# Four block owners packed into one word, read ahead of the marks; nine matmuls added to TensorE's stream at the end of attention

## The reference

```python
x = x + relu(attention(layernorm(x), ctx, ctx, mask) @ wo.T + wo_b)
h = layernorm(x)
weights, indices = gate(h)            # softmax over 32 experts, 4 of 8 groups, top 4 of 32
cw = scatter(weights, indices)        # [T, 32]
for e in range(32):
    y += cw[:, e] * ((silu(h @ w1[e] + b1[e]) * (h @ w3[e] + b3[e])) @ w2[e] + b2[e])
z = (silu(h @ sw1 + sb1) * (h @ sw3 + sb3)) @ sw2 + sb2
x = x + y + z
```

## Time and profile before

| | |
|---|---|
| time, median of 3 runs | 398.54 us (397.88 to 400.85) |
| time of the profiled execution | 398.79 us |
| its span, first to last instruction | 396.9 us |
| attention ends, the second part begins | about 159 us from the span's start |
| first row scatter to the last | 190.05 to about 231 us |
| marks landed | 239.7 us |
| first bias add of the block loop | 268.86 us |
| last bias add | 367.3 us |
| busy in the span | PE 288.5, DVE 222.1, POOL 181.8, ACT 147.2 us |

### The profile page before, as it was taken

One profiled execution on the slowest core, in us unless ns is written; L12 is line 12 of the kernel. 1 busy time (PEld: TensorE's weight loads), 2 busy tenths in 40 slices (PEclk: granted clock), 3 DMA queues, 4 the chain that ended last, 5 costly groups with the idle time before them and its releaser, 6 DMA issues.

```text
span 396.9 us, 7150 instructions
## 1 busy us (share of the span) xinstructions
PE 288.5 (73%) x2283; PEld 209.0 (53%) x2283; DVE 222.1 (56%) x702; ACT 147.2 (37%) x403; POOL 181.8 (46%) x188
## 2 busy tenths in 40 slices
PE   8899999999999994999910002207999999999200
PEld 3366666666666672947500002106778888888100
DVE  1778876777777775286940001004556666666277
ACT  1366666666667653231000000003444544444000
POOL 6466765756666750100677720001545555555400
PEclk9999999999999997589965555657999999999755
DMA  6868797787956000860133363001545555553394
GB/s 157 186 55 231 215 309 205 220 247 240 298 183 215 0 3 0 237 187 2 53 93 93 97 85 67 14 0 40 160 138 155 159 162 163 165 164 106 109 289 133
DMA packets 54013, 55.92 MB, mean 141 GB/s; under 512 B 18925, under 2 KB 45562, under 8 KB 53466
## 3 DMA queue, kind: packets, MB, share of 16 engines
q1 hardware_dynamic: 49610, 43.94, 40.4%
q0 software_dynamic: 4368, 11.52, 9.4%
HBM read 35.03 MB, written 20.41 MB: 140 GB/s over the span
## 4 chain that ended last, share of the span: by engine, by line
PE 24%; issue 19%; DVEq 6%; DVE 5%; DMA 3%; SPq 2%; POOL 1%; ACT 0%; POOLq 0%
PE ps L860 13%; PE ps L875 6%; DVEq L1078 6%; DVE x L1098 4%; PE ps L852 3%; PE ps L869 2%; DMA marks<-expert_rows 2%; SPq L735 1%; DMA b<-expert_out 1%; POOL expert_out L781 1%; DMA expert_out<-hs,to 1%; SPq L734 0%; DVE hh L1091 0%; ACT sg L932 0%; DVE hb L1085 0%
## 5 line engine op out<-in xcount | busy, mean ns | idle before, releaser
L286 POOL TENSOR_SCALAR z<-z,zmax 112x375 f32<-112x375 f32 x64 | 79.0, 1246 | 52.8 <-DVE zmax L546 52.8
L781 POOL DMA_INDIRECT expert_out<-hs,to x59 | 56.8, 962 | 84.9 <-DVE hs L1068 83.2
L546 DVE CUSTOM_DVE_ANT_0 z<-ps,mask_sb 112x375 f32<-112x375 f32 x128 | 62.5, 546 | 29.6 <-PE ps L365 29.6
L474 ACT ACTIVATE pT<-ps 125x336 f32<-125x336 f32 x128 | 50.7, 448 | 38.1 <-PE ps L342 37.7
L860 PE MATMUL ps<-w,xgT 128*128 x236 | 64.3, 396 | 0.5
L1085 DVE TENSOR_TENSOR hb<-ps,b 128x256 f32<-128x256 f32 x59 | 25.1, 425 | 60.1 <-issue 33.1
L342 PE MATMUL ps<-ident,z 112*125 112x112 f32 x384 | 56.6, 283 | 0.2 <-ACT pT L474 0.2
L852 PE MATMUL ps<-ident,xg 128*128 128x128 f32 x118 | 23.6, 285 | 45.4 <-issue 45.4
L342 PEld LDWEIGHTS ps<-ident,z 112*125 112x125 f32 x384 | 47.3, 188 | 15.4 <-ACT pT L474 7.3
L860 PEld LDWEIGHTS ps<-w,xgT 128*128 128x128 f32 x236 | 45.0, 197 | 11.0 <-issue 5.3
L776 POOL DMA_INDIRECT expert_rows<-normed,slots x32 | 32.0, 1000 | 39.1 <-DVE normed L1042 29.6
(11 more groups left out here) (156 smaller groups left out, 360.1 us busy)
## 6 DMA issues: line engine op xcount, KB each, us to landing
xg<-expert_rows SPq DMA_DIRECT2D x59, 128.0 KB
expert_rows<-zero SPq DMA_DIRECT2D x14, 512.0 KB, 10.0
w2s<-in_L_ffn_w SPq DMA_DIRECT2D x2, 2048.0 KB, 9.1
b<-in_L_ffn_b SPq DMA_DIRECT2D x2, 2048.0 KB, 12.9
b<-expert_out SPq DMA_DIRECT2D x8, 448.0 KB, 8.2
ctx_sb<-in_ctx SPq DMA_DIRECT2D x8, 375.0 KB
mask_sb<-in_mask_Bx1xSxS_ff SPq DMA_DIRECT2D x8, 164.1 KB, 2.4
expert_out<-hs,to POOLq DMA_INDIRECT x59
```

The costliest lines, as they stand in the source:

```text
L286: pool.tensor_scalar(z[:, n % RING, :], z[:, n % RING, :], zmax[:, n % RING:n % RING + 1], None, ALU.subtract).then_inc(by_pool, 1)
L474: nc.scalar.activation(pT[:, n % RING, :], ps[0:KP, T_BANK + at % 2, 0:KT * S], ACT.Exp).then_inc(ring_read, 1)
L546: nc.vector.tensor_tensor_reduce(out=z[:, n % RING, :], in0=ps[0:S, S_BANK + j, 0:SK], in1=mask_sb[:, b % 2, :], scale=-1.0 if j in ACT_HE ...
L781: pool.indirect_dma_start(ys, bass.IndirectOffsetOnAxis(ap=to[:, j:j + 1], axis=0), y_sb[:, j % 4, :], None).then_inc(y_sent[j % 4], 16)
```

## The change

Two parts. **Words:** the owners of four blocks are packed as digits of base 32 into one number below 32^4 (`word`, then `word_i` as integer). With 59 blocks there are NWORD = 15 words. Both engines read 15 words ahead of their loops and none in it; VectorE reads them in front of its wait for the marks. Each use of an owner now works it out from the word: `owner_of` shifts by 5, 10 or 15 bits and masks with 31, in front of the multiplication by the stride that `bass.ds` has had before. That is done for each of the two matmul calls of `up`, for `down`, and for the bias add. VectorE makes the words with four small memsets, one multiplication and one reduction more. PART, STEP and the rounding of NBLK keep their values (128, 32, 59). **Matmuls:** nine calls of `warm`, into a bank of PSUM whose scores have been read, stand between the last steps of attention on TensorE.

```diff
-    NBLK = (TOPK * T + E * (P - 1)) // P
-    LIM = -(-T // P)
+    PART = P
+    NBLK = -(-((TOPK * T + E * (PART - 1)) // PART) * PART // P)
+    NWORD = -(-NBLK * P // (4 * PART))
+    LIM = -(-T // PART)
+    STEP = 32
...
-                def warm(n):
+                def warm(n, bank=SUM_BANK):
...
+                pe.wait_ge(masked, HPQ * NQ)
+                warm(2, S_BANK)
                 turn_sums(B - 1)
+                warm(2, S_BANK)
                 turn_att(B - 1)
+                warm(1, S_BANK)
                 project(B - 1)
+                warm(4, S_BANK)
...
-            HELD = 44
+            def owner_of(words, n):
+                return (words[n // 4] >> (5 * (n % 4))) & (E - 1)
...
-                                               w13[:, k, bass.ds(own[j], 1), :].rearrange("p o c -> p (o c)"),
+                                               w13[:, k, bass.ds(owner_of(words, j), 1), :].rearrange("p o c -> p (o c)"),
...
-                                     w2s[:, bass.ds(own[j], 1), :].rearrange("p o c -> p (o c)"),
+                                     w2s[:, bass.ds(owner_of(words, j), 1), :].rearrange("p o c -> p (o c)"),
...
                 pe.wait_ge(table_ok, 1)
-                own = {j: pe.value_load(owner_i[0:1, j:j + 1], min_val=0, max_val=E - 1) for j in range(HELD)}
+                words = [pe.value_load(word_i[0:1, n:n + 1], min_val=0, max_val=E ** 4 - 1) for n in range(NWORD)]
...
-                    if j >= 2 and j - 2 + HELD < NBLK:
-
-                        own[j - 2 + HELD] = pe.value_load(owner_i[0:1, j - 2 + HELD:j - 1 + HELD], min_val=0, max_val=E - 1)
...
+                for f in range(4):
+                    nc.vector.memset(places5[:, f:f + 1], float(E ** f))
...
-                nc.vector.tensor_scalar(owner_i[:], owner[:], float(E - 1), None, ALU.min).then_inc(table_ok, 1)
+                chained(nc.vector.scalar_tensor_tensor(owner[:], owner[:], float(E - 1),
+                                                       places5[:].unsqueeze(1).to_broadcast([1, NWORD, 4]), ALU.min, ALU.mult))
+                chained(nc.vector.tensor_reduce(word[:], owner[:], AX.X, ALU.add))
+                nc.vector.tensor_copy(word_i[:], word[:]).then_inc(table_ok, 1)
...
+                dve.wait_ge(table_ok, 1)
+                words = [dve.value_load(word_i[0:1, n:n + 1], min_val=0, max_val=E ** 4 - 1) for n in range(NWORD)]
 
                 dve.wait_ge(marks_in, 16)
...
-                dve.wait_ge(table_ok, 1)
-                own = {j: dve.value_load(owner_i[0:1, j:j + 1], min_val=0, max_val=E - 1) for j in range(HELD)}
                 dve.wait_ge(scale_in, 16 * 2)
                 for j in range(NBLK + 3):
                     if j < NBLK:
-                        if j >= 1 and j - 1 + HELD < NBLK:
-                            own[j - 1 + HELD] = dve.value_load(owner_i[0:1, j - 1 + HELD:j + HELD], min_val=0, max_val=E - 1)
                         dve.wait_ge(up_done, j + 1)
                         TT(hb[:, j % 2, :], ps[:, U_BANKS[j % 2], 0:2 * INTER],
-                           b13[:, bass.ds(own[j], 1), :].rearrange("p o c -> p (o c)"), ALU.add).then_inc(biased, 1)
+                           b13[:, bass.ds(owner_of(words, j), 1), :].rearrange("p o c -> p (o c)"), ALU.add).then_inc(biased, 1)
```

More of the change, by code:

```diff
@@ L294, in _ @@
             def _(pe):
-                def warm(n):
+                def warm(n, bank=SUM_BANK):
                     for _ in range(n):
-                        nc.tensor.matmul(ps[:, SUM_BANK, :].rearrange("p (r c) -> p r c", c=P), ident[:],
+                        nc.tensor.matmul(ps[:, bank, :].rearrange("p (r c) -> p r c", c=P), ident[:],
                                          ident[:].unsqueeze(1).to_broadcast([P, BANK // P, P]), start=True, stop=True)
@@ L696, in experts @@
             cw = sbe("cw", [S, B, NE])
-            count1 = sbe("count1", [P, NBLK])
+            count1 = sbe("count1", [P, 4 * NWORD])
             copies = sbe("copies", [P, TOPK])
@@ L707, in experts @@
             gate = sbe("gate", [S, B, TOPK])
-            owner = sbe("owner", [1, NBLK])
-            owner_i = sbe("owner_i", [1, NBLK], I32)
+            owner = sbe("owner", [1, NWORD, 4])
+            word = sbe("word", [1, NWORD])
+            word_i = sbe("word_i", [1, NWORD], I32)
+            places5 = sbe("places5", [1, 4])
             hs = sbe("hs", [P, NSH, T])
@@ L958, in shared_h @@
                                                    sil[:, u % 2, :], ALU.add, ALU.mult).then_inc(hs_ok, 1)
-                chained(nc.vector.memset(over[:, 0:9, :], 1.0))
-                unit = over[:].rearrange("p e l -> p (e l)")[:, 0:NBLK]
+                for f in range(4):
+                    nc.vector.memset(places5[:, f:f + 1], float(E ** f))
+                chained(nc.vector.memset(over[:, 0:4 * NWORD // LIM + 1, :], 1.0))
+                unit = over[:].rearrange("p e l -> p (e l)")[:, 0:4 * NWORD]
                 chained(nc.vector.tensor_tensor_scan(count1[:], unit, unit, 0.0, ALU.mult, ALU.add))
                 chained(nc.vector.tensor_scalar(copies[:], count1[:, 0:TOPK], -1.0, None, ALU.add))
-                chained(nc.vector.tensor_scalar(full[:], count1[:, 0:LIM], -1.0, float(P), ALU.add, ALU.mult))
+                chained(nc.vector.tensor_scalar(full[:], count1[:, 0:LIM], -1.0, float(PART), ALU.add, ALU.mult))
                 dve.wait_ge(logits_ok, 1)
@@ L1033, in _ @@
                 chained(TT(blocks[:], ends[:], blocks[:], ALU.subtract))
-                chained(nc.vector.tensor_scalar(base1[:], blocks[:], float(P), 1.0, ALU.mult, ALU.add))
+                chained(nc.vector.tensor_scalar(base1[:], blocks[:], float(PART), 1.0, ALU.mult, ALU.add))
                 chained(TT(key[:], ps[0:S, 5, 0:B * E].rearrange("s (b e) -> s b e", e=E),
@@ L1042, in _ @@
                 nc.vector.tensor_scalar(normed[:, :, D:D + TOPK], best[:, :, 0:TOPK], -1.0, None, ALU.add).then_inc(slots_ok, 1)
-                for lo in range(0, NBLK, D * 4 // E):
-                    some = slice(lo, min(lo + D * 4 // E, NBLK))
+                for lo in range(0, 4 * NWORD, STEP):
+                    some = slice(lo, min(lo + STEP, 4 * NWORD))
                     n = some.stop - lo
@@ L1050, in _ @@
                                count1[0:1, some].unsqueeze(2).to_broadcast([1, n, E]), ALU.is_lt))
-                    chained(nc.vector.tensor_reduce(owner[:, some], passed, AX.X, ALU.add))
-                nc.vector.tensor_scalar(owner_i[:], owner[:], float(E - 1), None, ALU.min).then_inc(table_ok, 1)
+                    chained(nc.vector.tensor_reduce(owner[:].rearrange("p n f -> p (n f)")[:, some], passed, AX.X, ALU.add))
+                chained(nc.vector.scalar_tensor_tensor(owner[:], owner[:], float(E - 1),
+                                                       places5[:].unsqueeze(1).to_broadcast([1, NWORD, 4]), ALU.min, ALU.mult))
+                chained(nc.vector.tensor_reduce(word[:], owner[:], AX.X, ALU.add))
+                nc.vector.tensor_copy(word_i[:], word[:]).then_inc(table_ok, 1)
                 for r in range(TOPK):
```

## The result

The changed kernel takes **368.8 us** (median of four runs, 368.61 to 369.23) against 399.17 of the kernel before (four runs, 397.88 to 400.85): 0.926 of its time, interval 0.922 to 0.930. The profiled execution took 368.61 us, its span is 366.8 us. Of the kernels further down, words_only and dve_ahead each have one run in a slower state of the chip (373.88 and 371.10), which is left out of their times.

A forecast was written before the change was run, and what follows sets the result against it. It took GpSimd's scatters, VectorE's sequencer reading owners, then TensorE's block loop as the bound. Its terms gave 398.8 - 26.0 - 1.0 - 3.0 + 1.0 - 1.4 = 368.4 us, range 364.5 to 376.

The forecast's parts named there:

- Part 4: Shift and mask at each owner use in the block loop, taken as fused steps: plus 1.0 us, between 0 and 3.5.
- Part 5: Nine matmuls at attention's end: turn_sums later, +1.1; transposes and logits faster, -2.5; sum -1.4 us, between -2.5 and +1.1.
- Part 1: VectorE's owner reads moved ahead of the marks: first turn_h earlier by 26.0 us, between -25.2 and -26.7.
- Part 2: First blocks of the loop: less time with TensorE at half clock, minus 1.0 us, between -0.2 and -1.7.
- Part 3: No reads in the block loop: 14 blocks fall from 1.84 to 1.625 us, minus 3.0, between -2.7 and -3.2.
- rival (b): Shift and mask in the loop are not fused: 8.2 us in place of 1.0, so 375.6; chance 0.22.
- The rule: In the block loop, 0.22 us of register work stays unseen and half of what exceeds it is paid per block.
- The small ones: Four memsets and the words' three instructions, in VectorE's waiting time and beside GpSimd's scatters: no cost.
- Rival (a): Shift and mask in the block loop cost nothing: 367.4 us; chance 0.14.
- (c): The nine matmuls at the end of attention bring nothing and their +1.1 delay stays: 370.9 us; chance 0.12.
- (d): VectorE's early reads crawl to beyond the marks, until 247: +6, so 374 us; chance 0.05.
- (e): Slower than before: register work in the loop costs 0.52 us more a block, 399 us and more; chance 0.02.

The follow-up runs named there:

- words_only: The changed kernel without the nine matmuls; 371.72 us, 0.927 of the kernel before.
- dve_ahead: The changed kernel with VectorE's shift and mask put in front of its wait for up_done, TensorE unchanged; 366.47 us.
- words_late: The changed kernel with VectorE's 15 reads behind the marks' instructions, where the 44 stood; 377.85 us.
- ahead: The changed kernel with both engines' shift and mask put ahead of their waits; 366.64 us.
- fillers_only: The kernel before with the nine matmuls and nothing else; 395.55 us, 0.993 of the kernel before.
- move_only: The kernel before with VectorE's 44 reads in front of its wait for the marks, nothing packed, 15 reads left in the loop; 371.72 us.
- dve_double: The changed kernel with four register instructions on VectorE behind its wait for up_done, in place of one or two; 375.26 us.
- marks_late: ahead with the marks' DMA queued behind block 3's, and VectorE's wait and four instructions for them behind block 3's bias add; 365.18 us.
- best_fill: marks_late without the two matmuls in front of turn_sums; 364.21 us, 0.915 of the kernel before.

## Why the prediction was right

Forecast 368.4, measured 368.8; against the profiled executions, -30.4 forecast and -30.2 measured. The path was right: the reads out of the stall, block 1 next in line, the clock under the logits. That the sum hit within half a microsecond is luck. Part 4's loss was put too small by 2.0 and part 5's gain by 1.5; a stretch outside the change gave 0.8, and the scatters took 0.5. The ends of the terms were also added up wrongly: their worst ends give 398.8 - 25.2 - 0.2 - 2.7 + 3.5 + 1.1 = 375.3, not about 374.

- **Part 1, -26.0**: measured -25.6 from the last scatter to the first `turn_h`. TensorE and the landing of block 1 set it, as argued: block 1 landed 9.5 us behind the last scatter where 239.7 - 230.54 = 9.2 had been put. words_late gives the price of a read again, 0.635.
- **Part 2, -1.0**: half clock ends 0.96 us behind the first `turn_h`, not 3.6, so (3.6 - 0.96)/2 = -1.3, inside its bounds. The clock rose later behind the start of work than it had before: TensorE begins at 236.91, 5.3 us ahead of the rise, where 3.6 had been taken.
- **Part 3, -3.0**: it holds as a term. ahead, which has no reads and hidden register work, takes 92.92 us from the first `turn_h` to the last bias add where before took 97.31, 4.4 less. Half clock ends 0.5 behind the first `turn_h` in ahead, which gives (3.6 - 0.5)/2 = 1.5 of it; 2.9 are left for the reads.
- **Part 4, +1.0**: this step failed in its size. Its premise, a further *fused* step of 14 ns, was false: rival (b) was right that they are instructions of their own. That rival's 8.2 was too much. It counted the two steps again for `down`, which reuses the owner that `up` has worked out; its sizes for one use were near (0.17 on VectorE, by the records 0.16; 0.18 on TensorE, by the records 0.20). The 1.0 was too little: 58 x 0.052 = 3.0 us. So the packing gives back in the loop what leaving out the late reads brings, and parts 3 and 4 cancel: the same 50 distances have a mean of 1.676 before and of 1.677 after. The rule, half of both engines' sum less 0.22 unseen, gives (0.137 + 0.17 - 0.22)/2 = 0.04 with the sizes of the records, near the 0.052. But it would hide VectorE's part alone, which costs 0.031. The 0.22 was read off TensorE's slack and offered to both engines; VectorE's own air is some 0.075.
- **Part 5, -1.4**: this term was too small by 1.5. The +1.1 was exact, and the transposes went to 1.72. But the clock stayed for all of the logits, not half of them: 3.30 us, below even the 3.9 that I had put for full clock from the counts' rows. The bound of -2.5 was crossed (-2.9).
- **The small ones, nothing**: the scatters took 0.5 longer (below). In every kernel with words they take 40.9 to 41.0, in the three without 40.4 to 40.5. That belongs to the words.
- **Rival (a)**, by which the shift and the mask cost nothing (368.4 - 1.0 = 367.4), falls: 58 x 0.052 = 3.0 us is paid. TensorE's work alone costs 0.007 a block (dve_ahead), but beside VectorE's it costs 0.021. The chain that pays most is VectorE's: taking its work out of it brings 0.045 of the 0.052.
- **Rivals (c), (d), (e)** fall by fillers_only, by move_only with its 44 reads done at 227.6, and by the distance of 1.677.

Against before, packing is then 3.0 gained in late reads, 3.0 paid in shifts and masks, 0.5 paid in the scatters, and nothing at the marks that move_only doesn't have. The change was right for its second half, the place of the reads.

## What to carry to other kernels

Ask of a list of register reads first where it stands, then how long it is: put ahead of a wait that is long anyway (37 us here), 44 reads cost as little as 15 (371.72 us in move_only and in words_only), and the address work that the shorter list needed came back in the loop (0.052 us a block). Try register work in front of the semaphore wait, not behind it: here the same instructions in another place, with a copy of the register more, took 0.05 us off every block. When one stall of 27 us goes, look at what is queued on the same DMA queue as what comes last next; here the marks stood ahead of block 1. Moving them brought the first bias add 3.9 us forward, of which 3.1 came back in the loop.

## What the runs showed of the hardware that was not expected

**Reads that crawl, in some profiles only.** In after, VectorE's reads keep to some 0.65 us until about 204 and then lose their rhythm (source view of after; the 1 and the 700 ns are of those):

```profile
L1086 DVEq TENSOR_LOAD <-word_i x15: 1/306/700, 196.8 to 209.8; - x15
```

The same is seen from about 205 on in the earlier trace rows of before (TensorE), and in VectorE's last reads of dve_double (2 to 700 ns), marks_late (2 to 549) and best_fill (9 to 698). It isn't seen in the reads of move_only, which run through the same stretch on both engines until 227 (293 to 587 ns), nor in TensorE's of fillers_only, until 220 (293 to 585). It set no end in any of them. Only profiled executions can show it, and its cause stays open.

**Scatters beside VectorE.** A row scatter lasts 0.94 us and comes every 1.25. Beside the loop of three instructions that works out the gates (L1071 to L1073) some last longer (timeline of after):

```profile
190.66 0.94 POOL L789 DMA_INDIRECT expert_rows<-normed,slots  x1 [0.30 <-issue]
...
191.91 1.03 POOL L789 DMA_INDIRECT expert_rows<-normed,slots  x1 [0.30 <-issue]
...
192.62 0.43 DVE L1071 TENSOR_TENSOR mine<-key,best 112x256 f32<-112x256 f32 x1
193.08 0.42 DVE L1072 TENSOR_TENSOR mine<-mine,cw 112x256 f32<-112x256 f32 x1
193.25 1.07 POOL L789 DMA_INDIRECT expert_rows<-normed,slots  x1 [0.30 <-issue]
193.54 0.42 DVE L1073 TENSOR_REDUCE gate<-mine 112x8 f32<-112x256 f32 x1
```

Four gaps in a row become 1.34 to 1.38 us, the period of VectorE's three instructions being 1.37 (192.62 to 193.99). The same four gaps stand in every kernel with words; before, move_only and fillers_only have none above 1.27 there. That the words' own three instructions, by starting these later, put the scatters out of step is only argued.

**A clock that outlives the matmuls.** The nine end at 159.27 in after, 0.3 us before the transposes begin, and the granted clock stays at 1.00 through 16 transposes (1.72 us) and 32 thin matmuls (3.30), 5 us of work that had run at 0.50 throughout before (2.92 and 6.04).

**A rhythm of four.** The distances of bias adds after repeat with the digit's place: 1.54 into a block with a mask alone, 1.82 into the next, then 1.63 and 1.72 (means of twelve or thirteen). In ahead all four are 1.62 to 1.63.
